# Second cross-attention of a post-norm decoder: the output product in the second unit of a round, the next context's main part in the third

## The reference, cut to what matters

```
q = (x @ Wq).reshape(B, Tq, h, C) * SCALE
k = (context @ Wk).reshape(B, Tk, h, C) * SCALE
v = (context @ Wv).reshape(B, Tk, h, C)
attn = softmax(einsum('bqhc,bkhc->bhqk', q, k), axis=-1)
out = einsum('bhqk,bkhc->bqhc', attn, v).reshape(B, Tq, h * C)
return out @ Wo + bo
x = layernorm(x + L1_xattn(x, ctx_768))
x = layernorm(x + L1_ffn(x))
```

## Time and profile before

| | us |
|---|---|
| median of three runs | 997.63 |
| the profiled execution's own time | 994.54 |
| its span, first to last instruction | 992.7 |
| busy: TensorE matmuls / VectorE / ScalarE | 953.7 / 587.3 / 414.3 |
| second cross-attention, from 727 us to the end | 266 |
| output product starts, items 0 to 6 | 774.5, 803.7, 834.4, 865.8, 897.3, 926.5, 954.2 |

### The profile page before, as it was taken

How to read it: one execution, slowest core, us unless ns; L and a number is a source line. 1 busy time by engine, 2 the same in 40 slices (tenths; PEclk the granted TensorE clock), 3 DMA queues, 4 the chain that set the end, 5 groups by cost and what they waited for, 6 DMA issues and landing times. The chain is left out here.

```text
span 992.7 us, 17284 instructions
## 1 busy us (share of the span) xinstructions
PE 953.7 (96%) x6584; PEld 744.9 (75%) x6584; DVE 587.3 (59%) x1342; ACT 414.3 (42%) x1088; POOL 154.3 (16%) x151
## 2 busy tenths in 40 slices
PE   9899899999999999989999999999989999999975
PEld 4687777877878777768999998666657777767653
DVE  3788645555555565657756565368646454565554
ACT  3556534343343333436454545367643233232321
POOL 0333620110110100004443442300010000000000
PEclk9999999999999999999999999999999999999998
DMA  5500010000000000008511100720000000000000
GB/s 161 206 1 1 10 60 1 17 17 1 16 2 1 1 2 1 1 2 291 163 43 42 43 1 10 171 38 2 2 19 16 17 16 17 16 1 25 6 6 18
DMA packets 26825, 36.34 MB, mean 37 GB/s; under 512 B 3648, under 2 KB 22160, under 8 KB 26752
## 3 DMA queue, kind: packets, MB, share of 16 engines
q1 hardware_dynamic: 26752, 35.35, 12.1%
HBM read 30.75 MB, written 2.75 MB: 34 GB/s over the span
## 5 line engine op out<-in xcount | busy, mean ns | idle before, releaser
L1164 ACT ACTIVATE x_prob<-bank,x_negmax 112x375 f32<-112x375 f32 x128 | 72.2, 569 | 143.9 <-DVE x_negmax L1072 143.9
L1912 DVE TENSOR_TENSOR moe_h_low<-moe_sq,moe_h_high 128x512 fp32r<-128x512 f32 (+1 forms) x64 | 54.4, 871 | 50.6 <-ACT moe_h_high L2012 38.0
L1989 POOL TENSOR_TENSOR moe_sq<-moe_r 128x512 f32<-128x512 f32 (+1 forms) x64 | 64.2, 1006 | 102.8 <-ACT moe_r L2021 81.0
L1072 DVE TENSOR_REDUCE x_negmax<-bank 112x1 f32<-112x375 f32 x128 | 64.1, 542 | 9.5 <-PE bank L956 7.3
L2021 ACT ACTIVATE moe_r<-bank 128x512 f32<-128x512 f32 (+1 forms) x64 | 34.9, 545 | 72.6 <-PE bank L101 68.7
L101 PE MATMUL bank<-moe_w_low,moe_h_high 128*128 128x256 f32 x224 | 63.3, 283 | 0.0
L101 PE MATMUL bank<-moe_w_high,moe_h_low 128*128 128x256 f32 x224 | 63.3, 283 | 0.0
L101 PE MATMUL bank<-moe_w_high,moe_h_high 128*128 128x256 f32 x224 | 63.3, 283 | 0.0
L1077 DVE COPY x_prob_t<-bank 125x336 f32<-125x336 f32 x128 | 58.4, 497 | 2.9 <-PE bank L965 1.4
L956 PE MATMUL bank<-x_kt,x_qt 64*112 64x375 f32 x256 | 58.3, 521 | 1.2 <-issue 0.7
L1595 ACT ACTIVATE x_prob<-bank,x_negmax 112x375 f32<-112x375 f32 x64 | 36.1, 568 | 45.8 <-DVE x_negmax L1448 45.8
(11 more groups left out here) (377 smaller groups left out, 2365.5 us busy)
## 6 DMA issues: line engine op xcount, KB each, us to landing
moe_w<-in_L_ffn_W SPq DMA_DIRECT2D x15, 512.0 KB, 4.8
ctx_t<-in_ctx_t SPq DMA_DIRECT2D x8, 376.0 KB, 4.3
x_ctx_t<-in_ctx_t SPq DMA_DIRECT2D x8, 376.0 KB, 3.2
wk<-in_L_xattn_Wk SPq DMA_DIRECT2D x2, 1024.0 KB, 5.2
wv<-in_L_xattn_Wv SPq DMA_DIRECT2D x2, 1024.0 KB, 8.1
wq<-in_L_xattn_Wq SPq DMA_DIRECT2D x2, 1024.0 KB, 10.1
wo<-in_L_xattn_Wo SPq DMA_DIRECT2D x2, 1024.0 KB, 11.9
xt<-in_xt SPq DMA_DIRECT2D x1, 896.0 KB, 4.7
```

What stands on the lines that cost most here:

```text
L1072: dve.tensor_reduce(negmax[:, g:g + 1], S_BANK(u, e)[0:T, 0:S], AX_X, ALU.max, negate=True).then_inc(max_ready, 1)
L1164: act.activation(PROB(u, e)[:, :], S_BANK(u, e)[0:T, 0:S], ACT.Exp, bias=negmax[:, g:g + 1], accum_out=total[:, g:g + 1]).then_inc(p_ready, 1)
L1912: dve.tensor_tensor(h_low[half][:, m, 0:size], sq[m % 2][:, 0:size], h_high[half][:, m, 0:size].bitcast(F32), ALU.subtract).then_inc(low_d ...
L1989: pool.tensor_tensor(sq[m % 2][:, 0:size], r[m % 2][:, 0:size], r[m % 2][:, 0:size], ALU.mult).then_inc(sq_done, 1)
```

## The change

The two jobs change places, and VectorE's `residual` and ScalarE's `deviation` follow the output product into unit 1. `collect` of the first half keeps its place and its wait. No instruction is added or taken out.

```diff
         if u == 0 and at == LATE and i + 1 < B:
             return [(CTX_REST, i + 1)]
-        if u == 1 and at == LATE and i + 1 < B:
+        if u == 2 and at == LATE and i + 1 < B:
             return [(CTX_MAIN, i + 1)]
-        if u == 2 and at == LATE and i > 0:
+        if u == 1 and at == LATE and i > 0:
             return [(OUT, i - 1)]
...
-                        if u == 2 and i > 0:
+                        if u == 1 and i > 0:
                             residual(i - 1)
...
-                        if u == 2 and i > 0:
+                        if u == 1 and i > 0:
                             deviation(i - 1)
                         drain_all(jobs(i, u, LATE))
```

## The result

| | before | after | ratio (95% interval) |
|---|---|---|---|
| first comparison, 8 runs each | 999.74 us | 992.67 us | 0.9941 (0.9922 to 0.9959) |
| second comparison, 27 and 12 runs | 997.90 us | 993.45 us | 0.9960 (0.9941 to 0.9979) |
| the profiled execution's span | 992.7 us | 991.4 us | |

A forecast was written before the change was run, and what follows sets the result against it. TensorE was taken as the bound, busy 953.7 of 992.7 us, so only its gaps could close: 0.92 + 0.89 + 0.24 + 1.28 + 0.56 = 3.89 us, from the median 997.63 to 993.7 us, range 991.6 to 996.6.

The forecast's parts named there:

- rounds 2 to 5, unit 3: From the next item's first scores to BASE: `row_max` no longer held, 2.64 us becomes 2.41, 0.23 us in each round.
- round 6, units 1 and 3: Output product fills TensorE's wait ahead of scores(6,3), 0.89 us; the gap ahead of scores(7,1) shrinks by 0.24 us.
- round 7 to the last output product: Output product fills the wait between `turn` and scores(7,3), 1.28 us; NT of item 6 waits less for VectorE, 0.56 us.
- behind the last output product: The program's tail: TensorE's work there taken as unchanged, so no gain counted.
- The signs that I had named: Marks expected in the changed profile: `row_max` 0.1 us and BASE 2.4 us behind the scores, listed gaps closed or shorter.
- What the moved parts hold up: New waits behind `residual`, `deviation` and CTX_MAIN's copy in their new places: each 0, at most 0.3 us a round.
- one of run against run 1 us: Claimed uncertainty of one set of runs against another, 1 us, beside about 0.7 us for the sum itself.
- three of the signs meant to refute it: Idle ahead of `turn`, clock under 1.00 between 740 and 980 us, NT of item 6 less than 3 us earlier.
- slower, by the clock: Rival: new order brings one 1.7 us half-clock stretch in each of rounds 1 to 7, 1005.6 us; chance 0.05.
- the argument that an idle of 3.09 us in round 7 brought no fall: Argument against the slower-clock rival: TensorE's 3.09 us idle in round 7 left the clock up, and the change shortens idles.
- The sentence drawn from the Trainium skill: Short TensorE idles between matmul groups swing the clock; if so in rounds 6 and 7, 3.4 us more or less.
- Only the long gaps close: Rival: only rounds 6 and 7, unit 1, pay, 0.89 + 1.28 = 2.2 us, giving 995.4 us; chance 0.17.

The follow-up runs named there:

- late_only: The two jobs change places in rounds 6 and 7 alone, the other rounds as in the kernel before; median 993.7 us, ratio 0.9952 to the kernel before.
- before_again: The kernel before the change, run again without any edit; median 998.35 us, ratio 1.0 to the same kernel beside it.
- early_only: The two jobs change places in rounds 0 to 5 alone, rounds 6 and 7 as in the kernel before; median 996.6 us, ratio 0.9992 to the kernel before.
- after_again: The changed kernel, run again without any edit beside the kernel before; 993.45 us median, ratio 0.9960.
- both_in_2: Against the kernel before, only CTX_MAIN moves, so it and the output product are both in unit 2, the product first; 1000.40 us, ratio 1.0032.

## Why the prediction was right

The time, the sign and the mechanism were right. Term by term, from the same pair of traces, each span measured between the starts of the scores of unit 1 of successive rounds:

| step | forecast, us | measured, us |
|---|---|---|
| rounds 2 to 5, unit 3 | 0.92 (4 x 0.23) | 0.96 (0.22 to 0.26 each) |
| round 6, units 1 and 3 | 0.89 + 0.24 = 1.13 | 1.23 |
| round 7 to the last output product | 1.28 + 0.56 = 1.84 | 2.02, clock taken out |
| round 0 | not counted | 0.28 |
| behind the last output product | 0 | 0.32 |
| sum | 3.89 | 4.81; 4.4 over all runs at equal clock |

The 0.28 us over the forecast in rounds 6 and 7 is mostly `turn`. The sums put 0.75 us for it, but with the output product right behind it, it takes 918.80 - 918.12 = 0.68 and 945.28 - 944.63 = 0.65 us. The rest is VectorE's chain from the last `weigh` of round 7 to NT, 960.73 - 956.43 = 4.30 us where 4.37 was put.

The signs that I had named came out: 0.12 us from scores to `row_max`, 2.40 us to BASE, no idle ahead of scores(6,3) and scores(7,3), a gap of 0.15 us ahead of scores(7,1), 2.47 us of idle ahead of NT where 2.5 was said, and ScalarE's `collect` waiting for nothing but `weigh`:

```profile
PE bank L1382: 51.6, 16
```

*What the moved parts hold up* was taken at 0 and is: VectorE waited 0.79 us for the scores behind the residual chain, and TensorE's waits after hold no entry that they lacked before. The end's 0.32 us is the place of the last half-clock stretch, not the change's: in the trace of before it reaches into the LOW at 985.46, which takes 0.99 us, and in the one after it begins behind the same LOW, which takes 0.69. Round 0's 0.28 us is a gain that I had not counted, and nearly all of it is the change's. Behind `turn` the scores start after 744.37 - 743.72 = 0.65 us, where CTX_MAIN took 742.75 - 741.97 = 0.78 to start: 0.13. The first four score matmuls of the next round, now behind CTX_MAIN and no longer behind `weigh`, are shorter by 0.10. The half-clock stretch ahead of them accounts for the remaining 0.05. Traces of four executions with the old order in round 0 or the new one agree: 22.91 and 22.92 us for that round in late_only and before_again, 22.71 and 22.68 in early_only and after_again.

Three things in the prediction were not right. First, "one of run against run 1 us": the kernel before spreads over 992 to 1002 us, and the three runs that I started from could have had a median 2 us off. That 993.7 came so close to 992.67 and 993.45 owes something to luck: in the first comparison the medians lie 7.1 us apart, of which the forecast has 3.9, and it still lands within 1.0 us since the base of eight runs lies 2.1 us above the 997.63 that I started from.

Second, three of the signs meant to refute it appeared all the same. NT of item 6 is only 963.41 - 960.73 = 2.7 us earlier on the trace's own time; as the stage began 1.8 us late, it is 4.5 us earlier when measured from the first scores. An idle stands ahead of `turn` in round 7, 0.32 us at 944.63; the kernel before has the same 0.32 us at 945.30, so the change didn't bring it. And the clock is under 1.00 between 740 and 980 us, in round 0 (0.61 from 740.0 to 743.4) and in the last `weigh`; before_again has a stretch in both places too. So none of the three speaks against the change's own account, but as they were worded they would have refuted it. The signs should have been put as distances within the stage, and against more than one execution of before.

Third, the rival *slower, by the clock* was priced well at 1.7 us for a stretch, but I took a stretch as something that the new order brings. before_again shows that the old order has them too, at a mean clock of 0.990 against 0.9905. Its trace also answers the argument that an idle of 3.09 us in round 7 brought no fall: with 3.10 us in the same place the clock fell in the matmuls right behind it.

The sentence drawn from the Trainium skill ("TensorE: Matmul & The Clock Gate", "A second HAM failure mode: psum-queue depth-cycling"), that short idles between groups make the clock go to and fro, can't be settled either: early_only and both_in_2 keep the idles and have 0.990, late_only has fewer and 0.992, but the changed kernel has as few as that and 0.9905.

The range of 991.6 to 996.6 held both medians. *Only the long gaps close* is refuted by early_only's 1.1 us and by BASE, which comes 0.24 us sooner in each middle round.

## What to carry to other kernels

Where one engine is packed, look for the few places where it is not, and put the longest job that nothing waits for right there: here between a product and the softmax behind it, where a step of 1.98 us in two other engines had only 0.4 us or nothing over it. Pulling further work forward pays only into such gaps; in the packed rounds each microsecond moved is paid again. Before comparing two traces or two medians, take the clock out: in twelve runs of one kernel span times mean clock stayed within 1.3 us where the times spread over seven.

## What the runs showed of the hardware

- The same program takes between 994.2 and 1001.7 us in twelve runs (before_again). Its mean granted clock runs from 0.994 to 0.986 in them, and span times clock stays between 985.2 and 986.5 us.
- A stretch can fall or not in the same code: behind 3.09 us of idle there is none in the last `weigh` of the first profiled execution of before, and behind 3.10 us there is one in that of before_again, the same program.
- A group of four score matmuls takes 1.42 us behind CTX_MAIN, BASE or the output product, 1.43 behind `turn`, and 1.51 us behind a wait, behind `weigh` or behind CTX_REST (885.37 in the trace of before).
